# Low fp16 halves of the first weight chunks summed by TensorE instead of computed by VectorE, with a rebuilt end of the program, in a routed expert layer

## The reference

```python
masked_w = weight * mask[None, :, :]                      # (8, 256, 256)
w_bot = einsum('bg,got->bot', y, masked_w)                # one 256x256 matrix per batch
z = einsum('bnt,bot->bno', x, w_bot) + bias
xf = z.reshape(-1, 256)                                   # 2048 tokens
top1 = argmax(xf @ gate_w.T + gate_b, axis=-1)            # one of 8 experts
for e in range(8):
    h = relu(xf @ w1[e].T + b1[e])                        # 256 -> 1024
    y_e = h @ w2[e].T + b2[e]                             # 1024 -> 256
    out += where(top1 == e, y_e, 0)
return x + out
```

## Time and profile before

| what | value |
|---|---|
| median of 3 runs | 177.32 us |
| the profiled execution, its own time | 177.17 us |
| its span, first to last instruction | 174.8 us |
| PE busy | 156.8 us, 90% of the span |
| DVE busy | 120.8 us, 69% |
| ACT busy | 106.7 us, 61% |
| POOL busy | 61.9 us, 35% |
| DMA moved | 33.35 MB, mean 191 GB/s |

### The profile page before, as it was taken

One profiled execution on the slowest core, in us unless ns is written; L12 is line 12 of the kernel. 1 busy time (PEld: TensorE's weight loads), 2 busy tenths in 40 slices (PEclk: granted clock), 3 DMA queues, 4 the chain that ended last, 5 costly groups with the idle time before them and its releaser, 6 DMA issues.

```text
span 174.8 us, 6097 instructions
## 1 busy us (share of the span) xinstructions
PE 156.8 (90%) x1807; PEld 133.3 (76%) x1807; DVE 120.8 (69%) x225; ACT 106.7 (61%) x192; POOL 61.9 (35%) x59
## 2 busy tenths in 40 slices
PE   5999899994799999998978999999999999999720
PEld 2347588642689999997867999999999898888610
DVE  0496899957999979899999748989753543644000
ACT  3505988121899799699966578899536563453000
POOL 8200000058850226265187545662244220122220
PEclk9999999999999999999999999999999999999995
DMA  3999999957977889899978813222220100100000
GB/s 67 353 410 409 414 401 380 313 166 247 339 211 271 224 287 330 290 311 332 326 269 251 287 33 118 52 75 64 90 67 21 50 22 11 37 30 30 19 20 0
DMA packets 13791, 33.35 MB, mean 191 GB/s; under 512 B 2619, under 2 KB 6843, under 8 KB 13632
## 3 DMA queue, kind: packets, MB, share of 16 engines
q1 hardware_dynamic: 8288, 24.39, 40.1%
q0 software_dynamic: 2688, 6.30, 10.7%
q10 hardware_dynamic: 2784, 2.26, 3.9%
HBM read 30.06 MB, written 6.95 MB: 212 GB/s over the span
## 4 chain that ended last, share of the span: by engine, by line
PE 57%; DMA 21%; issue 10%; DVE 3%; DVEq 2%; POOL 1%; ACT 1%; SPq 1%; POOLq 0%; ACTq 0%
PE psum L913 22%; PE psum L897 18%; DMA wsp<-w_all 16%; PE psum L797 6%; PE psum L833 4%; PE psum L824 3%; DMA rows_in<-both_rows,tok_of_slot 2%; DMA both_rows<-stage 2%; PE psum L885 1%; DVE wsp L610 1%; PE psum L810 1%; PE psum L781 1%; DVE hT L718 1%; DVEq L610 1%; SPq L326 1%
## 5 line engine op out<-in xcount | busy, mean ns | idle before, releaser
L897 PE MATMUL psum<-xs,stage 128*128 128x128 f16 x1008 | 59.7, 219 | 2.2 <-ACT psum L509 1.1
L913 PE MATMUL psum<-wsp,hT 128*128 x504 | 58.5, 273 | 3.0 <-DVE hT L718 1.4
L897 PEld LDWEIGHTS psum<-xs,stage 128*128 128x128 f16 x1008 | 57.6, 98 | 3.8 <-issue 2.5
L913 PEld LDWEIGHTS psum<-wsp,hT 128*128 128x128 f16 x504 | 47.9, 98 | 10.1 <-issue 4.7
L413 POOL DMA_INDIRECT out<-rows_in,tok_of_slot x17 | 23.1, 1360 | 55.5 <-DVE rows_in L723 52.3
L408 POOL DMA_INDIRECT rows_in<-both_rows,tok_of_slot x17 | 25.2, 1480 | 39.7 <-issue 35.5
L610 DVE SCALAR_TENSOR_TENSOR wsp<-wsp x28 | 32.9, 1221 | 4.5 <-ACT wsp L492 4.3
L718 DVE SCALAR_TENSOR_TENSOR hT<-psum,hT 128x512 f16<-128x512 f32 x42 | 27.1, 683 | 11.7 <-ACT hT L526 11.7
L509 ACT ACTIVATE psum<-b_col 128x1024 f32 x21 | 21.5, 1023 | 16.3 <-issue 13.2
L492 ACT ACTIVATE wsp<-wsp x28 | 27.9, 1060 | 3.0 <-issue 2.6
L526 ACT ACTIVATE hT<-psum 128x512 f16<-128x512 f32 x42 | 22.7, 588 | 4.3 <-PE psum L897 4.2
(11 more groups left out here) (105 smaller groups left out, 99.4 us busy)
## 6 DMA issues: line engine op xcount, KB each, us to landing
wsp<-w_all SPq DMA_DIRECT2D x32, 512.0 KB
wsp<-cond_w SPq DMA_DIRECT2D x4, 512.0 KB, 6.8
wsp<-x_t SPq DMA_DIRECT2D x2, 1024.0 KB, 10.7
both_rows<-x_rows ACTq DMA_DIRECT2D x2, 1024.0 KB, 13.6
b_all<-b SPq DMA_DIRECT2D x1, 1024.0 KB, 17.4
both_rows<-stage SPq DMA_DIRECT2D x1, 768.0 KB, 7.0
both_rows<-stage SPq DMA_DIRECT2D x1, 512.0 KB, 5.8
both_rows<-stage SPq DMA_DIRECT2D x1, 384.0 KB, 4.6
```

Source lines behind the costliest of these rows:

```text
L897: last = t_.matmul(o, w1s[:, b, w:w + P], xs[:, b, xp, k * P:(k + 1) * P], start=False, stop=(c % 4 == 3 and k == KD - 1 and wp == 1), ski ...
L913: last = t_.matmul(ps_y[b], hT[:, b, hp, c * P:(c + 1) * P], w, start=False, stop=(c == KH - 1 and w is low), skip_group_check=True)
```

## The change

Five things change.

1. The low halves of chunks 0 to 3 are no longer computed by VectorE. TensorE adds `1 * raw` (an fp32 matmul with the identity as the stationary operand) and `-1/64 * hi` (an fp16 matmul) in two PSUM banks per chunk, and ScalarE casts the sum times 64 to fp16 (`low_out`, a PSUM read of 128x1024). For chunk 0 the raw part is cut in 16 pieces of 64 columns, one behind each of the small matmuls, in place of the matmuls of ones; for chunks 1 to 3 it is two matmuls of 512 columns. `low_out(0)` and `low_out(1)` stand ahead of ScalarE's wait for `experts_known`, `low_out(2)` and `low_out(3)` behind `x_hi(0, 0)`, followed by a wait for all four. All filling matmuls between the stages are gone.
2. `b2` is loaded behind the wait for the first gathered tile instead of right behind the first chunks.
3. GpSimd gets a `drain()` before the scatters of tiles 9, 12, 14 and 15 and before each scatter from tile 16 on.
4. The final waits for the stores move from GpSimd to SyncE, in nested branches.
5. TensorE's tile sequence for tiles 15 to 22 is written with one branch per tile, and the last used tile has its own code without a branch between its two `layer2`.

```diff
+DRAINS = (9, 12, 14, 15)
+        LOW_BANK = (1, 3, 5, 3)
             for q in range(CPE):
                 load_chunk(0, q)
-            sp.dma_start(b2_all[:, :, :], b2.partition_broadcast(P)).then_inc(ld_b2, 16)
...
             sp.wait_ge(x_in[0], 16)
+            sp.dma_start(b2_all[:, :, :], b2.partition_broadcast(P)).then_inc(ld_b2, 16)
             load_chunk(1, 2)
...
+            sp.wait_ge(experts_known, 1)
+            used = load_used(sp)
+            for i in range(SURE - RING, SURE):
+                sp.wait_ge(stored[i % RING], 16 * (i // RING + 1))
+            all_stored(SURE)
...
             def scatter(i):
+                if i >= SURE:
+                    pool.drain()
                 pool.wait_ge(y_ready, i + 1)
...
             for i in range(SLOT_TILES):
+                if i in DRAINS:
+                    pool.drain()
                 if_used(pool, used, i, lambda: scatter(i))
...
-            for i in range(SURE - RING, SLOT_TILES):
-                if_used(pool, used, i, lambda: pool.wait_ge(stored[i % RING], 16 * (i // RING + 1)))
...
+            a.mul(minus_ident[:, :], ident[:, :], -1.0 / WSCALE).then_inc(minus_ready, 1)
...
+            def low_out(n):
+
+                act.wait_ge(low_ps, n + 1)
+                a.mul(lo_of(n), psum[:, LOW_BANK[n]:LOW_BANK[n] + 2, :].rearrange("p q n -> p (q n)"),
+                      WSCALE).then_inc(lo_late, 1)
+
+            low_out(0)
+            low_out(1)
             act.wait_ge(experts_known, 1)
...
-            act.wait_ge(primed, 1)
+            act.wait_ge(lo_late, 1)
             seed_h(0, 0, plan.next_expert)
             x_hi(0, 0)
+            low_out(2)
+            low_out(3)
+            act.wait_ge(lo_late, EARLY)
             split_chunks(act, high_late, 0, plan.goal)
...
-            low(0)
-            low(1)
             dve.wait_ge(lo_late, CPL)
...
             x_lo(0, 0)
-            low(2)
-            low(3)
...
+            def raw_piece(t):
+
+                w = CH // TT
+                h, at = divmod(t * w, CH // 2)
+                t_.matmul(low_banks(0)[h][:, at:at + w], ident[:, :], place32(AHEAD)[:, t * w:(t + 1) * w],
+                          start=(at == 0), stop=False, skip_group_check=True)
+
+            def minus_high(n):
+
+                for h in range(2):
+                    last = t_.matmul(low_banks(n)[h], minus_ident[:, :], hi_of(n)[:, h * CH // 2:(h + 1) * CH // 2],
+                                     start=False, stop=True, skip_group_check=True)
+                return last
+
+            def low_sum(n):
+
+                pe.wait_ge(hi_ready, n + 1)
+                if LOW_BANK[n] in LOW_BANK[:n]:
+                    pe.wait_ge(lo_late, LOW_BANK.index(LOW_BANK[n]) + 1)
+                for h in range(2):
+                    t_.matmul(low_banks(n)[h], ident[:, :], place32(n + AHEAD)[:, h * CH // 2:(h + 1) * CH // 2],
+                              start=True, stop=False, skip_group_check=True)
+                minus_high(n).then_inc(low_ps, 1)
...
                     last.then_inc(tok_ps, 1)
-                else:
-                    t_.matmul(psum[:, 3, 0:D], ones_h[:, :], ones_h[:, :].unsqueeze(1).to_broadcast([P, 2, P]),
-                              start=True, stop=True)
+                raw_piece(t)
+            minus_high(0).then_inc(low_ps, 1)
             pe.wait_ge(rows_ready, TT)
...
-            keep_clock_up(24)
+            for n in range(1, EARLY):
+                low_sum(n)
             pe.wait_ge(experts_known, 1)
...
+            def last_tile(i):
+
+                layer1(i, i % 2)
+                layer2(i - 1, (i - 1) % 2)
+                layer2(i, i % 2)
...
+            for i in range(SURE - 1, SLOT_TILES - 1):
+                with pe.If(used > i + 1):
+                    turn_next(i)
+                    layer1(i, i % 2)
+                    layer2(i - 1, (i - 1) % 2)
+                with pe.Else():
+                    if_used(pe, used, i, lambda: last_tile(i))
```

More of the change, by code:

```diff
@@ L303, in load_used, with slot_tiles @@
             return eng.value_load(tiles_used[0:1, 1:2], min_val=SURE, max_val=SLOT_TILES)
-        def slot_tiles(eng, tile, plans=True):
-            plan = plans and Plan(eng, 0)
+        def slot_tiles(eng, tile):
+            plan = Plan(eng, 0)
             for i in range(SLOT_TILES):
@@ L416, in _ @@
             pool.wait_ge(pool_step, 3)
+            pool.wait_ge(x_stored, 32)
+            pool.wait_ge(routed, 1)
             for n in range(len(STORES)):
                 pool.wait_ge(rows_stored[n], 16)
[L419 to L420 removed]
             for i in range(RING):
@@ L859, in _, with low_banks @@
                 rows(t)
+            def low_banks(n):
+                return [psum[:, LOW_BANK[n] + h, :] for h in range(2)]
+            def raw_piece(t):
[16 more added lines that the diff above has]
+                minus_high(n).then_inc(low_ps, 1)
+            pe.wait_ge(minus_ready, 1)
+            pe.wait_ge(hi_ready, 1)
             for t in range(TT):
@@ L919, in _, with turn_next @@
             turn_x(0, 0, 0, 1)
-            keep_clock_up(4)
-            def tile(i, b, r, turn, plan=None):
-                if_used(pe, used, i + 1, lambda: turn_x(i + 1, 1 - b, (r + 1) % RING, turn + (1 if r == RING - 1 else 0)))
-                if_used(pe, used, i, lambda: layer1(i, b))
-                if late(i, 1):
-                    if_used(pe, used, i - 1, lambda: layer2(i - 1, 1 - b))
-            slot_tiles(pe, tile, plans=False)
-            i = SLOT_TILES - 1
-            if_used(pe, used, i, lambda: layer2(i, i % 2))
+            def turn_next(i):
+                turn_x(i + 1, (i + 1) % 2, (i + 1) % RING, (i + 1) // RING + 1)
+            def last_tile(i):
+                layer1(i, i % 2)
+                layer2(i - 1, (i - 1) % 2)
+                layer2(i, i % 2)
+            for i in range(SURE - 1):
+                turn_next(i)
+                layer1(i, i % 2)
+                if i >= 1:
+                    layer2(i - 1, (i - 1) % 2)
+            for i in range(SURE - 1, SLOT_TILES - 1):
+                with pe.If(used > i + 1):
+                    turn_next(i)
+                    layer1(i, i % 2)
+                    layer2(i - 1, (i - 1) % 2)
+                with pe.Else():
+                    if_used(pe, used, i, lambda: last_tile(i))
+            if_used(pe, used, SLOT_TILES - 1, lambda: last_tile(SLOT_TILES - 1))
 def kernel(x, cond_8, L0_cond_weight, L0_cond_mask, L0_cond_bias, L0_ffn_gate_w, L0_ffn_gate_b,
```

21 lines of the change are left out of this document (10 added, 11 removed).

## The result

The changed kernel takes **186.89 us** (median of 4 runs, 186.19 to 190.04), the kernel before took 177.28 beside it (176.75 to 179.02). The ratio is 1.051, with a 95% interval of 1.043 to 1.059: slower by some 9.6 us, where 175.5 was forecast and 179.4 was the upper end of the range. The profiled execution took 187.28 us, 185.5 of them the span, against 174.8 before. The time outside the span fell from 2.3 to 1.7 us, so the 10.7 us by which the span grew are 10.1 in the times of the two executions.

What follows compares the result with a forecast made beforehand. From 48 us on TensorE, then VectorE, then TensorE again were taken to bound the kernel, with an exposed start and end. 177.17 + 3.5 (start) - 0.4 - 1.1 (branches) - 3.7 (end) = 175.5 us, range 172.6 to 179.4.

Steps and rivals of the forecast that it cites:

- TensorE's branches: Term for TensorE's tile sequence: fewer branches a tile save 0.4 us in all, between 0 and 1.0.
- the last two `layer2`: Term at TensorE's last tile: without branches the next layer is ready at once, -1.1 us of a 1.16 us gap.
- TensorE pauses at a tile boundary after 134 us: Sign at TensorE's late tiles that would show the prediction wrong.
- The 0.25 us a tile: Step on TensorE: tiles take 5.81 us from 134 us on against 5.56 earlier, put down to three branches.
- long jumps stall: Rival: TensorE's five jumps over the last tile's copy; three pay, +4.5 us, 180 us in all; chance 0.08.
- The end: Term behind the last scatter: short drains at 0.08 us per DMA, the span ends with the last landing, -3.7 us.
- a drain takes over 2 us: Sign on GpSimd that would show the prediction wrong; drains of under a microsecond were expected.
- The rival with 3.50 a drain: Rival on GpSimd's end: each drain costs 3.50 us whatever is before it, 179.7 us in all; chance 0.12.
- The start: Term up to `layer1(1)`: ScalarE's extra casts and wait delay it from 47.92 to 51.5, +3.5 us, bounds +1.6 to +5.
- VectorE's relief: Step in the early part: VectorE loses four low halves of 1.22 us, but this is not on the path.
- The clock: Rival before `layer1(1)`: TensorE's idle gap halves its clock, the layer takes 2.7 us more, 178.2 us; chance 0.18.
- without a pause in which a late start could be made good: Claim on the kernel from 48 us on: TensorE, VectorE, then TensorE set the time, so a late start stays.

Runs made afterwards that it cites:

- d1: The changed kernel with the copies of the last tile's code moved behind all tiles: 196.26 us, ratio 1.101.
- g1: The kernel before with c1's end and, from tile 16 on, one TensorE branch whose else part holds 24 matmuls: 175.65 us, ratio 0.987.
- c1: The kernel before with SyncE's final waits and GpSimd's drains ahead of scatters 16 to 20, without the four early drains: 173.94 us, ratio 0.978.
- a3: a1 with 13 filler matmuls put back on TensorE ahead of `layer1(1)`: 176.37 us, ratio 0.986.
- a1: The changed kernel with TensorE's tile sequence of before, three short branches a tile: 178.2 us, ratio 0.993.
- b4: The kernel before with only the low halves on TensorE and ScalarE, b2 moved and the fillers gone: 180.76 us, ratio 1.017.
- a2: The kernel before with only TensorE's new tile sequence: 185.7 us, ratio 1.042.
- a4_end_again: The kernel before with only GpSimd's drains, early ones included, and SyncE's final waits, run again for a second profile: 174.07 us, ratio 0.980.
- f1: c1 with one early drain back, ahead of scatter 9: 175.76 us, ratio 0.990.
- after: The changed kernel itself, with all five changes, against the kernel before: 186.89 us, ratio 1.051.
- after_again: The changed kernel, unchanged, run again for a second profile: 187.2 us in one execution.

## Why the prediction was wrong

**TensorE's branches** are the step that failed. The prediction put them at -0.4 and the last two `layer2` at -1.1. The second came true: the two follow each other with 0.18 us idle, not 1.16. The first was +7.6 with it, so that alone carries the time beyond the range. "TensorE pauses at a tile boundary after 134 us" was also one of its own signs of being wrong. The 0.25 us a tile that were to be saved are there: `d1`, as long as it has no long jump, gains 1.3 us on the kernel before from `layer1(13)` to `layer2(18)`, and `g1` 1.35 on `c1`. The argument was that jumps over one layer's code stay within 0.33 us, and it was carried over to jumps over 96 matmuls, twice as long. The rival "long jumps stall" named the mechanism, at 0.08. Three things were off in it. The size: 2.4 - 0.9 = 1.5 us a jump, by a DMA's landing less the lead of the queue, where 1.9 to 2.9 was measured between layers and 3.1 to 3.2 behind the last. The number: three of the five jumps over the copy were let pay; two of them did, but the jump into the else part of the last tile was not counted, and the cheap ones left pauses inside the next layer. And the place: the jumps over the unused tiles, behind the last matmul, were in no case. The rule of the Trainium skill, "Runtime: NRT & Kernel Launch", section "Instruction fetch mechanics", that a taken branch to a block outside the window waits for its fetch, agrees with these rows: every jump of over 1 us ended 1.3 to 1.5 us behind the end of a packet of instructions. The weight given to it was wrong: the trace of before has no jump that far whose target is needed on the path, so its 0.33 us spoke neither for nor against, and a price with nothing against it can't stand at 0.08.

**The end** was put at -3.7. Alone it measures -3.65 from the last matmul on, so the size was right, but by luck, since the reason was not. A drain was taken at 0.08 us, and takes 2.1 to 7.1; "a drain takes over 2 us" was the second of its signs. It was harmless because GpSimd idles for nearly 5 us ahead of each late scatter, and because the last drain of 2.1 lies beside the landing of 2.4 that is waited for in any case. The rival with 3.50 a drain was nearer in size and failed for the same cover: the drain ahead of the last scatter takes 2.38 and holds its instruction back by only 0.2 us. In the changed kernel the end gave 1.2 in place of 3.65, since TensorE's last jumps took its place. That was the sum's second gap: when a stall of 3.5 us is taken away, every engine's tail is to be looked at.

**The start** was put at +3.5 and measured +2.8 (3.1 alone). Each step was met within 1.0 us, the last small matmul within 0.2. The farthest was `x_hi(1)`, at 46.42 and not 47.4: the 1.59 us read from the earlier trace rows as the queue's time for the branches hold the 0.63 of `x_hi(0)` itself and 0.96 of waiting for TensorE, and behind the casts ScalarE's idle time was 1.26. As said, VectorE's relief brought nothing: ScalarE's two casts and its wait for all four low halves stand ahead of `seed_h(1)`.

**The clock** fell, which had 0.18. The pause was 3.58 us where 4.2 was expected, and it fell 1.1 us after `layer1(1)` had begun; the cost was 1.2 and not 2.7, as only a part of the layer ran at half speed. `a3` shows that the pause is the cause: without it the clock stays up.

**Beyond 48 us** the prediction had "without a pause in which a late start could be made good". The stretch that VectorE sets gave 0.8 back in both profiles of the changed kernel. VectorE's relief isn't the reason: `a1`, `a3`, `b4` and `d1` have it too and got back less than 0.1. Nearly all of it falls on one tile, from `layer1(8)` to `layer1(9)`, which takes 6.9 us in the kernel before and in those four, 6.2 in the changed kernel, and 6.3 in `a2`, `a4_end_again` and `f1`, which have no relief. Why isn't known.

Terms measured: +2.8 + 1.2 - 0.8 + 1.0 + 7.6 - 1.2 = +10.6, against the span's +10.7, from which they differ by rounding. Without the new tile sequence the kernel stands at 0.993 of before (`a1`), some 176.0 us; the forecast without its two terms for this part is 177.0.

## What to carry to other kernels

Price a branch by the code that it jumps over and by the work that stands between it and the jump before, and look if a packet of instructions ends shortly ahead of its end: short jumps in a trace say nothing of one over a copied tile, and a copy in an else part is paid for by the path that doesn't take it. When a tail is removed from one engine, list when each of the others is done, code without work included. A wait or a drain is free only while its engine has idle time in front of the next work, so its duration and its cover are two questions.

## What was not expected of the hardware

- Five jumps over 96 matmuls in a row took 2.5 to 3.3 us each, with six instruction packets in 17 us; with a tile's work between them the same jumps took 0.19 to 1.95, with up to 1.2 us of pause later, inside a layer. Jumps over 72 to 74 matmuls took 0.22 to 0.44 or 2.4 to 3.4, jumps over 24 took 0.17 to 0.22. All 23 jumps of over 1 us ended 1.31 to 1.49 us behind the end of an instruction packet.
- GpSimd's DRAIN took 2.1 to 2.6 us with one indirect DMA since the last, but 3.6 to 4.7 in six cases of this kind (`after`, `after_again` and `g1`). It took 2.95 to 7.10 with four or more, 3.50 with 42 that had all landed and 4.23 with the last of them still under way.
- TensorE's clock fell to 0.50 only 1.1 us after work had begun again behind a pause of 3.58 us, and was full again at 55.2 us, 3.4 us later. `b4`, with 3.53 us, shows the same, and in `a1`, with 3.59 us, it fell 0.7 us ahead of the layer; with the pause filled it stayed at 1.00.
